# Copying the next group's indices on VectorE instead of GpSimd, in an attention and mixture-of-experts kernel

## What is computed

```python
x = x + _L0_xattn_ref(_layernorm(x, axis=-1), ctx_1024, ctx_1024)
x = x + _L0_ffn_ref(_layernorm(x, axis=-1), router_w, w1, b1, w2, b2)

# in _L0_ffn_ref
logits = jnp.einsum('th,eh->te', x, router_w)
topk_logits, topk_idx = jax.lax.top_k(logits, K)          # K = 2 of E = 8
probs = jax.nn.softmax(topk_logits, axis=-1)
hmid = gelu(jnp.einsum('th,efh->etf', x, w1) + b1[:, None, :])
y = jnp.einsum('etf,ehf->eth', hmid, w2) + b2[:, None, :]
out = jnp.einsum('eth,te->th', y, combine)
```

## Time and profile before

| | us |
|---|---|
| median of 3 runs | 854.59 (853.89 to 854.79) |
| the profiled execution, its own time | 850.98 |
| its span in the trace | 849.2 |

### The profile page before, as it was taken

The page is one execution under the profiler, slowest core; times in us unless marked ns, Lnnn a source line. Parts: engine busy times, 40 slices in busy tenths (PEclk is TensorE's granted clock), DMA queues, the critical chain, the costliest instruction groups (busy, mean ns, idle before and its releaser), DMA issues. The chain is left out here.

```text
span 849.2 us, 22604 instructions
## 1 busy us (share of the span) xinstructions
PE 751.6 (89%) x5931; PEld 642.1 (76%) x5932; DVE 622.8 (73%) x1520; ACT 388.0 (46%) x716; POOL 565.4 (67%) x737
## 2 busy tenths in 40 slices
PE   6999998799999544999999899999789999999995
PEld 5778886678878443997888787889569887878775
DVE  6998999899999777876666566466356665666664
ACT  3555666376776611444443443234234434434432
POOL 5664777688887305667767777646677676776774
PEclk9999999799999656999999999889899999999998
DMA  7887875368887602445544545534444344344340
GB/s 236 252 261 238 240 226 158 122 206 268 270 266 253 208 17 75 143 160 156 167 149 149 167 153 161 156 101 118 128 139 135 119 126 132 102 128 132 106 133 5
DMA packets 82200, 137.20 MB, mean 162 GB/s; under 512 B 10075, under 2 KB 55140, under 8 KB 82032
## 3 DMA queue, kind: packets, MB, share of 16 engines
q0 software_dynamic: 23104, 68.43, 26.9%
q1 hardware_dynamic: 59056, 68.26, 25.8%
HBM read 94.56 MB, written 47.59 MB: 167 GB/s over the span
## 5 line engine op out<-in xcount | busy, mean ns | idle before, releaser
L1062 ACT ACTIVATE work<-psum,b1T 128x256 f32<-128x256 f32 x312 | 130.7, 470 | 289.0 <-PE psum L682 288.9
L705 PE MATMUL psum<-w2T_high,slots 128*128 x1248 | 212.8, 276 | 15.8 <-issue 9.4
L682 PE MATMUL psum<-work,w1T_high 128*128 128x256 f16 x1248 | 211.7, 275 | 2.5 <-ACT work L1070 2.5
L705 PE MATMUL psum<-w2T_low,slots 128*128 x624 | 172.1, 276 | 0.0
L682 PE MATMUL psum<-work,w1T_low 128*128 128x256 f16 x624 | 171.6, 275 | 0.0
L954 DVE CAST slots<-work 128x512 f16<-128x512 f32 x156 | 70.2, 450 | 116.9 <-ACT work L1062 114.9
L705 PEld LDWEIGHTS psum<-w2T_high,slots 128*128 128x128 f16 x1248 | 117.8, 99 | 38.1 <-issue 23.9
L682 PEld LDWEIGHTS psum<-work,w1T_high 128*128 x1248 | 122.8, 99 | 18.1 <-issue 2.9
L563 PE MATMUL psum<-slots,work 128*128 (+1 forms) x512 | 123.4, 391 | 6.7 <-ACT slots L993 5.9
L528 POOL DMA_INDIRECT slots<-rows_first,slots x86 | 93.5, 1087 | 52.1 <-POOL slots L506 25.9
L563 PEld LDWEIGHTS psum<-slots,work 128*128 128x128 f32 x512 | 93.9, 192 | 31.3 <-issue 15.4
(11 more groups left out here) (125 smaller groups left out, 1108.7 us busy)
## 6 DMA issues: line engine op xcount, KB each, us to landing
work<-in_ctx SPq DMA_DIRECT2D x96, 256.0 KB, 3.5
rows_first<-slots SPq DMA_DIRECT2D x32, 514.0 KB, 3.9
slots<-in_x SPq DMA_DIRECT2D x32, 256.0 KB, 3.9
work<-in_L_ffn_w SPq DMA_DIRECT2D x32, 256.0 KB, 3.2
work<-in_x SPq DMA_DIRECT2D x32, 256.0 KB, 3.1
slots<-rows_first,slots POOLq DMA_INDIRECT x86, 3.7
rows_second<-slots POOLq DMA_INDIRECT x78
slots<-rows_second,slots POOLq DMA_INDIRECT x78, 3.6
```

The source lines that it names most:

```text
L682: mm = pe.matmul(h, w1T[pw][:, f, c, bass.ds(e * P, P)], xT[r2][:, (px * HC + c) * GROUP:(px * HC + c + 1) * GROUP], start=(c == 0 and px ...
L705: mm = pe.matmul(y, act16[r2][pa][:, f * GROUP + s * P:f * GROUP + (s + 1) * P], w2T[pw][:, f, bass.ds(e * DIM, DIM)], start=(f == 0 and p ...
L1062: last = act.activation(act32[r2][:, f * GROUP:(f + 1) * GROUP], psum[:, 2 + 2 * r2 + f // 2, (f % 2) * GROUP:(f % 2 + 1) * GROUP], ACT.Ge ...
```

## The change

GpSimd no longer copies indices. VectorE copies them for group i+1 in the same step i, between its second low half (group i-3) and its bias (group i-3), with the same wait for the lane's stores. The first copy (group 0) now stands behind the placing of round 2's tokens (`place_tokens(1)`) and the wait for the scaled bias. The waits for the list are gone, since VectorE makes the list itself.

```diff
@@ gpsimd
-            pool.wait_ge(r_index, 1)
-
-            def indices_of(g, r):
-
-                pool.tensor_copy(ring_idx[:, r * 4:r * 4 + 4], index[:, bass.ds(g * 4, 4)]).then_inc(x_idx, 1)
-
-            indices_of(0, 0)
-
             def group(i, k, n, rnd):
...
-                if live(i, k, -1, ALL):
-
-                    if is_step(i, k, GROUPS - 1):
-                        pool.wait_ge(r_index, 2)
-                    after(pool, x_out[(k + 1) % LANES], n * 32 + (k + 1) // LANES * 32)
-                    indices_of(i + k + 1, (k + 1) % LANES)
             expert_steps(pool, group)
@@ vector
+            def indices_of(g, r):
+
+                dve.tensor_copy(ring_idx[:, r * 4:r * 4 + 4], index[:, bass.ds(g * 4, 4)]).then_inc(x_idx, 1)
+
+            indices_of(0, 0)
+
+
             def group(i, k, n, rnd):
...
                         dve.tensor_tensor(act16[r2][1][:, cols], act32[r2][:, cols], act16[r2][0][:, cols], ALU.subtract).then_inc(x_low, 1)
+                if live(i, k, -1, ALL):
+                    after(dve, x_out[(k + 1) % LANES], n * 32 + (k + 1) // LANES * 32)
+                    indices_of(i + k + 1, (k + 1) % LANES)
+                if live(i, k, L_G1, ALL):
                     if not is_late(g):
                         add_bias(g, r, n * 32 + (k - L_G1) // LANES * 32 + 32, round_of(i, k, L_G1, rnd))
```

## The result

The changed kernel takes 951.31 us (median of 4 runs, 949.98 to 954.5); the kernel before took 854.24 us on the same chip (4 runs). The ratio is 1.115, its 95% interval 1.111 to 1.119: slower by 97 us. The profiled execution has a span of 949.2 us, against 849.2 before, so the two traces differ by the same 100 us that have to be explained.

The account below looks back on a forecast made before the run. GpSimd and TensorE were both taken as close to the bound. Rounds +60.8 and +36.5, start +3, list +1, round change 0, tail -6 give +95.3; with 850.98 and 3.61, rounded to 950 us, range 915 to 985 (0.80).

Parts of the forecast that it names:

- The ring: VectorE's copy waits for scatters its previous last operation released, ahead of the next: 8.05 us a step, second round 7.5.
- The links: From VectorE's last operation: first scatter 0.92 (second round 1.07), second scatter 1.39 (1.4), landing 3.07 (2.3), next last operation's end 2.7 us.
- the sum: All terms of the expert stage added: 60.8 + 36.5 + 3 + 1 + 0 - 6 = +95.3 us.
- The list stop: Making the second round's list, 13.6 us longest wait, fits nearly whole into TensorE's idle time; VectorE's part adds +1 us.
- What GpSimd would gain: GpSimd loses the copy and the gap behind it: 0.9 us less per step, from 6.69 to some 5.8 us.
- the third rival: Faster: store landed by VectorE's low half, so GpSimd's 5.8 and TensorE's 5.63 us set the pace; 831 us, chance 0.03.
- The start: First index copy and first gather now stand behind the placing of the second round's tokens: +3.0 us.
- The short and the long ring: Rivals: stores land in 2.1 to 2.5 us, 890 to 915 us, 0.08; casts slow GpSimd's descriptors, 985 to 1,006, 0.05.
- The lower clock: Steady stretches: TensorE's busy share was to fall to about 0.75 to 0.8 at a clock of 1.00.
- rival 4: TensorE, idle some 1.7 us in every step, falls to half clock, 11.3 us a step: 1,180 us, chance 0.02.

## Why the prediction was right, point by point

- **The ring decides.** Right, and shown three ways: the copy's place, the number of buffers, and the chain of waits. It was read out of the kernel before, where the wait cost nothing, by asking for each wait which instruction releases it and whether that instruction now stands behind the waiting one.
- **The links.** L967's end to the first scatter was taken as 0.92 and 1.07 us, measured 0.90 (the last operation before it started at 472.38 and took 0.87; the scatter starts at 474.15) and 0.91. First to second scatter 1.39 and 1.4, measured 1.35 and 1.34. Landing: 3.07 in the first round, where the page's list of DMA issues after gives a median of 2.9; 2.3 in the second, where the turn shown has 2.35, its neighbours 2.45 and the list of issues a median of 2.5; that is the 0.1 by which this ring was too short. Landing to the end of the last operation 2.7, measured 2.73 in the chain. The first round's ring was so 0.1 us too long (8.05 against 7.95 a step), the second's 0.1 too short (7.5 against 7.60); the errors nearly cancel in the sum. The list stop fitted into the ring almost whole, as argued: four steps of 8.6 to 9.1 us stand around it, and two of 6.8 and 5.3 us behind it.
- **What GpSimd would gain.** The 0.9 us per step was there, and none of it reached the time, since GpSimd waits 3.1 us for VectorE in each step. It was real: with the ring open, the same relief is worth 35 us, more than the 24 us that the third rival gave it. The step could reach 5.7 us, where that rival had 5.8.
- **The start** was the term mis-sized: +3 predicted, +7.4 in the traces, of which about 5.3 belong to the change. The term counted only the copy's delay and not what the gathers behind it would then fall beside. The row that tells it was in the trace of before (a gather of 2.85 us at 330.14, next to one of 0.95), but I had not read it as a price.
- **The number** is closer than the sum. The traces differ by 100.0 us, and the sum said 95.3. To it were added the 3.61 us by which the profiled run of the kernel before lay below its median; the profiled run of the changed kernel, 951.0 us, lies 0.3 us below its own. That 950 met 951.31 so closely is luck: single terms are off by up to 5 us in either direction, and the offset did not return.
- **The short and the long ring.** Neither came. With the gathers behind the scatters the landing takes a median of 2.9 us in the first round, hardly less than the 3.07 of the one row before, and scatters next to VectorE's casts took 1.05 us, hardly more than the 1.01 before.
- **The lower clock.** The forecast named a clock of 1.00 for the steady stretches; that was wrong for parts of both rounds, though far from the half clock of rival 4. It costs next to nothing in the steady steps. The table by stretches after:

```profile
440.00:480.00 40.00, 32.21 (x272) 26.14 (x270) 19.88 (x46) 13.30 (x25) 20.29 (x20) 0.91 0.39 124
480.00:520.00 40.00, 32.42 (x304) 27.44 (x302) 20.27 (x48) 14.25 (x27) 20.28 (x20) 1.00 0.40 125
...
604.00:608.00 4.00, 4.00 (x26) 4.00 (x25) 1.32 (x4) 0.00 (x0) 0.98 (x1) 0.50 0.45 130
...
760.00:800.00 40.00, 32.68 (x305) 27.52 (x304) 20.93 (x50) 14.18 (x27) 21.16 (x21) 1.00 0.36 106
```

The same busy share, about 0.8, stands at 0.91 in the first stretch and at 1.00 in the next and in the one of the second round. TensorE waits for the ring in all three, so the slower matmuls fill idle time: the five steps from 440.92 to 480.56 take 7.93 us each, the five from there to 519.75, at the full clock, 7.84. In the second round they are no shorter than a landing of 2.5 instead of 2.9 us explains. One step is different. While TensorE makes the list of round 2, it is busy throughout and its clock falls to 0.50 (604 to 608 us); in the step from 607.65 to 616.30 VectorE waits 3.42 us for activations and its copy, at 615.20, for no store. There TensorE sets the pace and the clock can cost something, at most the 0.7 us by which this step is longer than 7.95.

The Trainium skill's fit for a GpSimd-issued transfer (page "DMA: Bandwidth & Descriptors", section "Anatomy of one DMA — SWDGE (gpsimd) path") gives 2.6 and 2.3 us as an estimate; measured from a scatter's start the landing takes 2.9 and 2.5 (medians). It is near, and slightly short for both; with 2.6 in place of 3.07 the first round's ring would have been 7.61 us against a measured step of 7.95, and its loss too small by about 13 us (38 x 0.34).

## What to carry to other kernels

When a wait moves to another engine, follow its releaser: if the release comes from that same engine and the next release stands behind the wait, the full round trip (dispatch, transfer, landing, and all work between wait and release) becomes the least length of a step. Put the wait behind the release in the stream, or add a buffer so that it concerns an older transfer; either made this change worth 35 us instead of a loss of 97. A trace in which a wait never bites does not say that it is free in another place, but its rows hold every link from which the price can be summed.

## What the hardware showed that was not expected

- A long half-precision operation of VectorE holds up GpSimd's indirect transfers and copies beside it: two gathers took 2.73 and 2.29 us instead of 0.95, and in the kernel before a copy of 4 numbers per partition took 2.23 us instead of 0.19. The copy ended at 329.34, 0.05 us after VectorE's operation:

```profile
326.53 2.76 DVE L892 TENSOR_TENSOR slots<-slots 128x4992 f16<-128x4992 f16 x1
327.11 2.23 POOL L506 COPY slots<-slots 128x4 int32<-128x4 int32 x1
```

  The low half L956 did the same to the index copy of the kernel before. The copy at 468.54 took 0.64 us and ended at 469.18, 0.04 us after this one:

```profile
468.45 0.69 DVE L956 TENSOR_TENSOR slots<-work,slots 128x512 f16<-128x512 f32 x1
```

  So the copy that this change took off GpSimd cost more there than its own 0.19 us: 0.29 us as the median of its 79 times. Beside the last operation L970, which reads PSUM, it took 0.20 to 0.22 us. The Trainium skill, page "GPSIMD Engine Reference", section "1. Specifications", says that GpSimd shares its SBUF interfaces with VectorE and that instructions with two SBUF inputs contend; the long operation has two, and the trace agrees with it. The low half has two as well. It held up the copy, but scatters beside it took 1.05 us instead of 1.00 and a gather 1.31 instead of 0.98 (with low half and bias of the earlier trace rows beside it); how far one kind of instruction is held up and another is not, that sentence does not tell.
- From the landing of a transfer to VectorE's next f32 operation behind a register load it takes 1.05 us, though the copy in between starts after 0.16 us. With the 0.91 us from the last operation's end to the first scatter, that is more than a quarter of the ring's 7.33 us.
